# Query and cross-attention biases moved into TensorE products, first norm folded into the output projection: one change to a fused decoder layer on one core

## The reference

```python
q = x @ Wq.T + bq
...
q = jax.nn.softmax(q, axis=-1)          # inside each head of 16 channels
k = jax.nn.softmax(k, axis=-2)
state = jnp.einsum('bhnd,bhne->bhde', k, v)
out = jnp.einsum('bhnd,bhde->bhne', q, state)
mu = out.mean(-1, keepdims=True)
var = out.var(-1, keepdims=True)
out = (out - mu) * jax.lax.rsqrt(var + EPS) * ln_g + ln_b
return out @ Wo.T + bo
...
logits = jnp.einsum('bhqd,bhkd->bhqk', Q, K) + b[0]
logits = logits + -1e+30 * (1.0 - mask)
weights = jax.nn.softmax(logits, axis=-1)
...
x = _layernorm(x + attn(x))
x = _layernorm(x + xattn(ctx, x))
x = _layernorm(x + ffn(x))
```

## Time and profile before

| | us |
|---|---|
| median of 3 runs | 1266.06 (1258.21 to 1266.71) |
| span of the profiled execution | 1256.1 |
| TensorE busy | 1096.2 (87%) |
| VectorE busy | 764.7 (61%) |
| GpSimd busy | 645.5 (51%) |
| ScalarE busy | 495.2 (39%) |

### The profile page before, as it was taken

One profiled execution on the slowest core, in us unless ns is written; L12 is line 12 of the kernel. 1 busy time (PEld: TensorE's weight loads), 2 busy tenths in 40 slices (PEclk: granted clock), 3 DMA queues, 4 the chain that ended last, 5 costly groups with the idle time before them and its releaser, 6 DMA issues.

```text
span 1256.1 us, 27061 instructions
## 1 busy us (share of the span) xinstructions
PE 1096.2 (87%) x8572; PEld 904.3 (72%) x8572; DVE 764.7 (61%) x1863; ACT 495.2 (39%) x913; POOL 645.5 (51%) x736
## 2 busy tenths in 40 slices
PE   6568977878887699988899999999999999999960
PEld 3345665656655488877788888888888888888750
DVE  2667978987897687754844444444444444444326
ACT  3754534544343255553233333333333333333214
POOL 3012317756673777766775455555555555554324
PEclk9878979979896799998999999999999999999985
DMA  6421223222212333433444654555544445563326
GB/s 176 154 91 59 93 75 104 74 65 80 77 38 64 72 62 76 71 64 68 65 76 77 134 85 77 77 77 77 77 77 77 77 77 77 77 77 60 64 55 243
DMA packets 163039, 105.07 MB, mean 84 GB/s; under 512 B 107596, under 2 KB 153856, under 8 KB 162656
## 3 DMA queue, kind: packets, MB, share of 16 engines
q1 hardware_dynamic: 132896, 67.67, 21.4%
q0 software_dynamic: 30016, 35.68, 19.7%
HBM read 51.91 MB, written 36.04 MB: 70 GB/s over the span
## 4 chain that ended last, share of the span: by engine, by line
PE 65%; DVE 15%; POOL 9%; issue 5%; DMA 3%; ACT 3%; SPq 0%; POOLq 0%; ACTq 0%; DVEq 0%
PE big L1663 25%; PE big L1682 13%; PE trans L1682 11%; PE big L1705 3%; POOL slot_records L779 3%; PE big L1604 2%; PE small L1751 2%; PE small L1615 2%; POOL early_sums L809 2%; PE trans L1533 2%; POOL rstd L755 1%; PE small L1583 1%; PE big L1707 1%; DVE stat L1047 1%; DVE w_down L1043 1%
## 5 line engine op out<-in xcount | busy, mean ns | idle before, releaser
L1663 PE MATMUL big<-xgT,w_up 128*128 128x256 f16 (+1 forms) x3456 | 408.0, 267 | 12.7 <-DMA xgT<-xg 10.1
L1663 PEld LDWEIGHTS big<-xgT,w_up 128*128 x3456 | 324.7, 98 | 55.9 <-issue 16.4
L902 ACT ACTIVATE h<-big,up_scale 128x512 f32<-128x512 f32 x270 | 185.5, 687 | 451.4 <-PE big L1663 437.6
L1296 DVE TENSOR_SCALAR hh<-h,h_scale 128x512 f16<-128x512 f32 x270 | 133.8, 496 | 312.5 <-ACT h L902 310.8
L809 POOL DMA_INDIRECT token_sums<-y,rec x99 | 163.2, 1649 | 244.5 <-ACT y L910 223.5
L1682 PE MATMUL big<-w_down,hh 128*128 x1264 | 216.8, 274 | 2.8 <-DVE hl L1298 2.5
L1298 DVE SCALAR_TENSOR_TENSOR hl<-h,h_scale,hh 128x512 f16<-128x512 f32 x270 | 203.0, 752 | 9.6
L1682 PE MATMUL big<-w_down,hl 128*128 x632 | 173.0, 274 | 0.0
L1682 PE MATMUL trans<-w_down,hh 128*128 x896 | 152.8, 273 | 2.6 <-DVE hl L1298 2.4
L779 POOL DMA_INDIRECT slot_records<-recs,posi x128 | 130.2, 1017 | 35.3 <-issue 33.6
L1682 PEld LDWEIGHTS big<-w_down,hh 128*128 128x128 f16 x1264 | 123.2, 98 | 20.8 <-issue 3.8
(11 more groups left out here) (249 smaller groups left out, 1512.4 us busy)
## 6 DMA issues: line engine op xcount, KB each, us to landing
w_down<-in_L_ffn_up_w_dram SPq DMA_DIRECT2D x8, 1024.0 KB, 5.0
w_down<-in_L_ffn_down_w_dram SPq DMA_DIRECT2D x7, 1024.0 KB, 5.7
XA<-in_x_dram SPq DMA_DIRECT2D x32, 128.0 KB, 2.6
XRES<-in_x_dram SPq DMA_DIRECT2D x32, 128.0 KB, 2.4
token_rows<-XR SPq DMA_DIRECT2D x32, 128.0 KB, 1.8
sums<-token_sums SPq DMA_DIRECT2D x8, 512.0 KB, 7.2
out_dram<-sums SPq DMA_DIRECT2D x8, 512.0 KB, 2.6
xgT<-xg SPq DMA_TRANSPOSE x135
```

What stands on the lines that cost most here:

```text
L902: act.activation(h[:, i % H_RING, :], psu[up_bank(i)], ACT.Gelu_apprx_tanh, scale=k["up_scale"][:, t:t + 1]).then_inc(gelu_ready, 1)
L1296: dve.tensor_scalar(hh[:, i % HALF_RING, :], h[:, i % H_RING, :], k["h_scale"][:, t:t + 1], None, ALU.mult).then_inc(hh_ready, 1)
L1663: ins = pe.matmul(psu[up_bank(i)][:, j * size(t):(j + 1) * size(t)], w[:, ws, c, m:m + P], xgT[:, t % 2, xs * CC + c, 0:size(t)], start=(n ...
```

## The change

The query bias is split into three bf16 rows (`query_bias_rows`, once, on VectorE) and added by a fourth product per tile, of ones with these rows, into the query columns of the PSUM tile. `take_qkv` then takes the maximum and the difference straight from PSUM. The mask operands `one16` and `mbf` become 128 partitions high: row 0 still holds the mask, rows 1 to 3 hold the three bf16 parts of the scalar bias (`context_bias_rows`), the rest is zero; so `logit_shift` goes and `shifted_logits` only subtracts. The first norm is no longer applied to `Z`: the rows of the projection are centred once (`center_projection`, with a product for the means in step 1), and the reciprocal deviation is applied in `first_sum`. The deviation of `Z` is worked out as before, but only `first_sum`, a step later, waits for it.

```diff
-        mbf = sb("mbf", [1, XPC, KEYS], BF16)
-        one16 = sb("one16", [1, P], BF16)
+        mbf = sb("mbf", [P, XPC, KEYS], BF16)
+        one16 = sb("one16", [P, P], BF16)
+        bq16 = sb("bq16", [P, C], BF16)
...
             done(pool.memset(one16[:, :], 1.0))
+            done(pool.memset(mbf[:, :, :], 1.0))
...
-                    act.wait_ge(qs_ready, a + 1)
+                    act.wait_ge(big_free, BIG["qkv", a] + 1)
                     act.activation(Q[:, a % TB, :], Q[:, a % TB, :], ACT.Exp).then_inc(qe_ready, 1)
...
+            def center_projection():
+
+                mean = small_wait(("wm",))
+                for c in range(CC):
+                    dve.wait_ge(woT_ready, c + 1)
+                    ins = dve.scalar_tensor_tensor(out=woT[:, c, :], in0=mean[:, 0:C], scalar=-1.0 / C, in1=woT[:, c, :], op0=ALU.mult, op1=ALU.add)
+                ins.then_inc(sm_free, 1)
...
-                dve.tensor_tensor(Q[:, i, :], src[:, 2 * C:3 * C], bias[:, 0:C], ALU.add).then_inc(big_free, 1)
-                q3 = Q[:, i, :].rearrange("p (h d) -> p h d", h=LH)
-                dve.wait_ge(big_free, BIG["qkv", g] + 1)
-                dve.tensor_reduce(qm[:, g % 2, :], q3, AX_X, ALU.max).then_inc(qm_ready, 1)
+                new = src[:, 2 * C:3 * C].rearrange("p (h d) -> p h d", h=LH)
+                dve.tensor_reduce(qm[:, g % 2, :], new, AX_X, ALU.max).then_inc(qm_ready, 1)
...
-                dve.tensor_tensor(q3, q3, qm[:, g % 2, :].unsqueeze(2).to_broadcast([P, LH, LD]), ALU.subtract).then_inc(qs_ready, 1)
+                dve.tensor_tensor(Q[:, i, :].rearrange("p (h d) -> p h d", h=LH), new, qm[:, g % 2, :].unsqueeze(2).to_broadcast([P, LH, LD]), ALU.subtract
+                                  ).then_inc(big_free, 1)
...
-                dve.tensor_tensor(X1[:, g % 3, :], y_[:, 0:C], XRES[:, g % 2, :], ALU.add).then_inc(sm_free, 1)
+                dve.wait_ge(rstd_ready[0], g + 1)
+                dve.scalar_tensor_tensor(out=X1[:, g % 3, :], in0=y_[:, 0:C], scalar=rstd[:, 0, g % 4:g % 4 + 1], in1=XRES[:, g % 2, :],
+                                         op0=ALU.mult, op1=ALU.add).then_inc(sm_free, 1)
...
-            def logit_shift(g):
+            def shifted_logits(g):
                 dve.wait_ge(xm_ready, g + 1)
-                dve.tensor_scalar(xmb[:, g % 2, :], xm[:, g % 2, :], bcol[:, 0:1], None, ALU.add).then_inc(xmb_ready, 1)
...
-                dve.scalar_tensor_tensor(out=pr[:, :, :], in0=logit_view(g), scalar=bcol[:, 0:1],
-                                         in1=xmb[:, g % 2, :].unsqueeze(2).to_broadcast([P, XH, KEYS]),
-                                         op0=ALU.add, op1=ALU.subtract).then_inc(big_free, 1)
+                dve.tensor_tensor(pr[:, :, :], logit_view(g), xm[:, g % 2, :].unsqueeze(2).to_broadcast([P, XH, KEYS]), ALU.subtract
+                                  ).then_inc(big_free, 1)
...
+                if s == MEANS_STEP:
+                    center_projection()
+                    context_bias_rows()
...
-                if c0 is not None:
-                    norm(0, c0, Z[:, :], z_ready)
-                if c2 is not None:
-                    logit_shift(c2)
...
-                    pe.wait_ge(z_ready, c1 + 1)
+                    pe.wait_ge(sm_free, SM["out", c1] + 1)
                     turn("z", c1, Z[:, :])
...
-                        ins = pe.matmul(dst[:, 2 * C:3 * C], xT[:, c, :], wqkv[:, c, 0:C], start=(c == 0), stop=(c == CC - 1))
-                    ins.then_inc(big_ready, 1)
+                        pe.matmul(dst[:, 2 * C:3 * C], xT[:, c, :], wqkv[:, c, 0:C], start=(c == 0), stop=False)
+                    if a == 0:
+                        pe.wait_ge(query_bias, QUERY_BIAS_STEPS)
+                        pe.wait_ge(consts, MASK_MADE)
+                    pe.matmul(dst[:, 2 * C:3 * C], one16[:, :], bq16[:, :], start=False, stop=True).then_inc(big_ready, 1)
+                if s == MEANS_STEP:
+                    pe.wait_ge(woT_ready, CC)
+                    for c in range(CC):
+                        ins = pe.matmul(small_into(("wm",))[:, 0:C], ones[:, :], woT[:, c, :], start=(c == 0), stop=(c == CC - 1))
+                    ins.then_inc(sm_ready, 1)
```

More of the change, by code:

```diff
@@ L87 @@
 LAG = 2
+MEANS_STEP = 1
 HALF_RING = 4
@@ L356, in layer @@
         bcol = sb("bcol", [P, 1])
+        bpart = sb("bpart", [P, 4])
+        bhalf = sb("bhalf", [P, 2], BF16)
         kmx = sb("kmx", [P, C])
@@ L1018, in _, with query_bias_rows @@
                 dve.tensor_scalar(kdiag[:, c, :], ones[:, :], gb[:, 1, c:c + 1], None, ALU.mult).then_inc(lnbb_ready, 1)
+            def query_bias_rows():
+                bq_ = bias[:, 0:C]
+                rest, high, mid = X1[:, 0, :], X2[:, 0, 0:P].bitcast(BF16), X2[:, 0, P:C].bitcast(BF16)
+                dve.tensor_copy(high, bq_).then_inc(query_bias, 1)
+                dve.wait_ge(query_bias, 1)
+                dve.tensor_tensor(rest, bq_, high, ALU.subtract).then_inc(query_bias, 1)
+                dve.wait_ge(query_bias, 2)
+                dve.tensor_copy(mid, rest).then_inc(query_bias, 1)
+                dve.tensor_scalar(bq16[:, :], high, ident[:, 0:1], None, ALU.mult).then_inc(query_bias, 1)
+                dve.wait_ge(query_bias, 4)
+                dve.tensor_tensor(rest, rest, mid, ALU.subtract).then_inc(query_bias, 1)
+                dve.scalar_tensor_tensor(out=bq16[:, :], in0=mid, scalar=ident[:, 1:2], in1=bq16[:, :], op0=ALU.mult, op1=ALU.add).then_inc(query_bias, 1)
+                dve.wait_ge(query_bias, 6)
+                dve.scalar_tensor_tensor(out=bq16[:, :], in0=rest, scalar=ident[:, 2:3], in1=bq16[:, :], op0=ALU.mult, op1=ALU.add).then_inc(query_bias, 1)
@@ new lines, in context_bias_rows, with done @@
+            def context_bias_rows():
+                high, mid = bhalf[:, 0:1], bhalf[:, 1:2]
+                rest, sum1, sum2, sum3 = (bpart[:, i:i + 1] for i in range(4))
+                n = [0]
+                def done(ins):
+                    n[0] += 1
+                    ins.then_inc(context_bias, 1)
+                    dve.wait_ge(context_bias, n[0])
+                done(dve.tensor_copy(high, bcol[:, :]))
+                done(dve.tensor_tensor(rest, bcol[:, :], high, ALU.subtract))
+                done(dve.tensor_copy(mid, rest))
+                done(dve.tensor_tensor(sum1, high, ident[:, 1:2], ALU.mult))
+                done(dve.scalar_tensor_tensor(out=sum2, in0=mid, scalar=ident[:, 2:3], in1=sum1, op0=ALU.mult, op1=ALU.add))
+                done(dve.tensor_tensor(rest, rest, mid, ALU.subtract))
+                done(dve.scalar_tensor_tensor(out=sum3, in0=rest, scalar=ident[:, 3:4], in1=sum2, op0=ALU.mult, op1=ALU.add))
+                dve.wait_ge(consts, MASK_MADE)
+                done(dve.tensor_scalar(mbf[:, :, :], mbf[:, :, :], sum3, None, ALU.mult))
+                assert n[0] == CONTEXT_BIAS_STEPS
@@ L1019, in _ @@
+            query_bias_rows()
             for c in range(CC):
```

28 lines of the change are left out of this document (15 added, 13 removed).

## The result

The changed kernel takes **1246.13 us** (median of 4 runs, 1242.32 to 1250.27) beside 1264.49 for the kernel before (4 runs, 1258.21 to 1266.71): a ratio of 0.9855, 95% interval 0.9821 to 0.9889. The prediction was 1247. A second measurement with more runs gave 1245.64 and a ratio of 0.9881 [0.9847, 0.9915]. The profiled execution of after is the slowest of its four, and that of before lies near the lowest of its runs, so the two spans differ by 7.8 us only (a second profile of the changed kernel has a span of 1242.2 us); a difference between the two traces is therefore read in the place where it arises, not at the end.

The account below looks back on a forecast made before the run. TensorE binds some of steps 0 to 48, VectorE others; experts' products bind from about 590 us. 8.5 - 1.9 + 6.6 + 8.9 + 2.0 - 0.8 = 23.3, less 4.4, leaves 19 us: 1266.06 to 1247, range 1231 to 1259.

Parts of the forecast that it names:

- the first term: Mask product on TensorE made 128 rows high: 0.5 us a tile in 17 tiles, 8.5 us won.
- The mask product: On TensorE, from 0.23 to about 0.13 us, f32 pairs behind it from 0.71 to about 0.52; 8.5 us won.
- Rival 1: Mask product on TensorE saves nothing because a 128-row load waits as the one-row load did: 1256 us, chance 0.12.
- The norm of `Z`: VectorE norm removed, so TensorE's turning no longer waits for it: 8.9 us won, 4.9 of it in steps 10 and 11.
- The query add and the shift: VectorE passes removed: add 6.6 us won, its replacement product on TensorE 1.9 lost; shift of the maxima 2.0 won.
- A quarter: Deduction of 4.4 us from the VectorE terms (query add, norm, shift; 17.5), since GpSimd's residual-sum deviation comes next.
- rival 2: GpSimd takes over in batches 2 and 3 and the mixed stage; about 11 us won, 1255 us, chance 0.16.
- Rival 3: PSUM tile held 0.8 us longer by VectorE, so TensorE waits in all 32 tiles: 1273 us, chance 0.03.
- Rival 4: TensorE's clock stays at 2.4 GHz without the `Z` waits, 2 to 4 us more in steps 10 to 12: 1239, chance 0.06.
- Setup: Extra one-time VectorE passes and TensorE's product for the means: 0.8 us lost, from 0.3 to 2.
- VectorE's busy time: Expected profile sign: falls some 36 us over 32 tiles, less 5 for the setup.
- The residual sum's scalar: On VectorE, the scalar operand the residual sum gains was set against the one the shifted logits lose.

## Why the prediction was right in its number and wrong in its sum

The number held: 1247 predicted, 1246 measured. The mechanism of the first term held too. But the sum that led to the number had one term that is zero as the kernel stands, two that were too small, and a wrong rule for putting them together. That the number came out is in part luck. The 22.6 us that the parts cost when they are undone one by one stand beside the sum's 23.3 because the norm's miss is made up by the others. And the 19 us were taken off 1266.06, the median of three runs; the larger sets of the kernel before have 1260.03 to 1261.99, so that the same 19 us would have led to 1241 to 1243.

**The mask product: right in its mechanism.** 0.13 and 0.52 us, a step of 9.16 where 9.2 to 9.3 was foretold, 7.8 us by the run with the one-row product, where the sum had 8.5. The count of 17 tiles hit by luck: in the kernel in whose chain they were counted the edit wins nothing, and the chain of the kernel after holds five. Rival 1 is out. By the rule of the Trainium skill ("TensorE: Matmul & The Clock Gate", section "Why this matters for your kernels") that a single product of few rows takes as long as one of 128, that run would have cost nothing. For the product by itself the traces agree (0.30 us long in the timeline before, 0.29 after, with modelled ends); for this stream of products the measurement decides against it, since a product and the pair behind it follow at 0.23 and 0.71 us with one row and at 0.13 and 0.52 with 128.

**The norm of `Z`: the step that failed.** The prediction said of steps 10 and 11 that "the next thing in TensorE's queue is ready: 4.9 won", and set 8.9 in all. The waits did go, but the next thing was not ready. In the queue of the same step stands the product for a weight piece's scale, which waits for a transfer and ScalarE's square; before, that wait lay hidden behind the one for `Z`. By the run with the norm again, 4.4 us still came through to the first logits; one step later 1.0 was left: there the changed kernel's TensorE waits 2.25 us for ScalarE's copy of the turned `Z`, behind VectorE's split of the piece and GpSimd's two deviations. In the other steps VectorE's idle time for the deviation of the residual sum took the norm's place. By the times the norm costs 0.35 us when it is put back (to within some 6), and taking it alone out of the kernel before wins nothing (to within some 3). Once the piece is moved it costs 6.3 us by the ratios, and turning the order of GpSimd's two deviations gives 5.7. Those last gains belong to the edits that follow, not to the change as it stood. Why the kernel before, with the norm alone taken out, loses its early lead between 200 and 310 us stays open.

**The query add and the shift: too small.** 9.1 and 5.3 us by the runs that undo them, where the sum had 6.6 - 1.9 = 4.7 and 2.0. They were counted by the pieces that they had on the chain of the kernel before. But with TensorE's step 0.49 us shorter, more steps close on VectorE and GpSimd. The shift has 16 pieces there instead of 7, which account for 3.7 of the 5.3 us; its place behind the norm of `X` in that run has a part in them that was not separated. For the query add the chain explains the first half only.

**Putting the terms together: wrong.** A quarter was taken off all three VectorE terms. By the runs that undo them one lost everything and two lost nothing, and the terms are not independent. Taken back one at a time out of the changed kernel, the mask, the query add, the shift and the norm cost, by the medians, 7.8 + 9.1 + 5.3 + 0.35 = 22.6 us, more than the whole change wins (14.4 in that measurement, 18.4 in the first one). The mask alone wins nothing, all without it 0.58%. The likely reason is argued, not shown by a run of its own: in the kernel before, TensorE's chain and that of VectorE and GpSimd are so nearly equal that shortening one of them alone is worth next to nothing, and in the changed kernel lengthening either again costs most of its length.

**The rivals.** GpSimd (rival 2) was half right: its two deviations in a row bind more steps than before, as the waits and the run with their order turned show, but the mask's 7.8 us came through all the same, and 1255 did not come. The gain was not lost in the mixed stage, where rival 2 looked for part of it. Rival 3 did not happen: TensorE shows no wait for VectorE before its products into the big banks (L1653, L1754). Rival 4's mechanism is there, 3.29 us down to 1.88, but the clock falls again behind the wait for the square (0.50 from 89 to 91 us), and 1239 did not come. **Setup**: the first state product starts at 70.3 instead of 69.6 us, 0.7 where 0.8 was counted; but in the second profile of the same kernel it starts at 71.3, so one profile can't tell. **VectorE's busy time** fell by 26.3 us where 31 was foretold; the lengths of its operations, counts times means of all groups, fell by 31.6 (830.5 to 798.8). The count was right, then: the page counts only once the time in which an operation runs into its neighbour. The residual sum's scalar (15.2 us instead of 13.3) and the logits' lost one (25.3 instead of 27.3) do cancel, as was foretold.

## What to carry to other kernels

When a trace shows an engine waiting, look at what stands next in the same queue and when *that* is ready, a transfer or a weight piece included: the wait is worth only the distance to the second latest, and one step further the same question comes again. Where two chains are nearly equal, undo parts from the finished version as well as adding them to the old one; a part that is worth nothing alone can carry half the gain in company. And when an operation is taken away that had covered another engine's latency, look whether the order on that engine was chosen for the old cover.

## What the runs showed of the hardware

A bf16 product of one row between f32 passes of 128 rows costs 0.23 us and makes the following pair cost 0.71; with 128 rows, of which 124 are zero, it costs 0.13 and the pair 0.52. Filling an operand up with zeros paid here, though only where TensorE's products set the pace. The Trainium skill ("TensorE: Matmul & The Clock Gate", section "The mechanism") says that weight loads overlap a running product only when their row groups differ, or when they go to the background weight buffer. Here the full-height load runs ahead of its product, and in front of the load of one row the loads stood still for 0.42 us; the row groups alone would not tell these two apart, and which buffer a load goes to no run here shows. And on GpSimd a deviation of 128 by 1, one value a partition, takes 0.21 to 0.39 us for the sum and 0.57 for the power, so that two in a row are some 1.9 us from the first sum's start to the second power's end (138.30 to 140.19), longer than any VectorE pass over 256 elements beside them.
